# Packed columns for the third tile of 32 experts, its place in the order, and a subtraction in two pieces

## The reference

```python
E, K, F = (32, 4, 352);  FS = 1408;  CAP = 256
# every token goes to 4 of 32 experts; an expert takes at most 256 rows
buf = zeros((E, CAP + 1, H)).at[sorted_e, dest].set(x[tok])[:, :CAP]
g = einsum('ech,ehf->ecf', buf, w_gate)
u = einsum('ech,ehf->ecf', buf, w_up)
y = einsum('ecf,efh->ech', silu(g) * u, w_down)
out = zeros((T, H)).at[tok].add(y[sorted_e, pos] * wv)
out = out + sigmoid(x @ w_shared_gate) * (silu(x @ sw_gate) * (x @ sw_up) @ sw_down)
```

## Time and profile before

| | us |
|---|---|
| median of 3 runs | 1687.3 (1687.01 to 1688.22) |
| the profiled execution | 1695.61 |
| its span, first to last instruction | 1693.8 |
| TensorE matmuls busy | 1647.0 |
| VectorE busy | 1272.6 |
| GpSimd busy | 836.7 |
| ScalarE busy | 697.7 |

### The profile page before, as it was taken

One profiled execution on the slowest core, in us unless ns is written; L12 is line 12 of the kernel. 1 busy time (PEld: TensorE's weight loads), 2 busy tenths in 40 slices (PEclk: granted clock), 3 DMA queues, 4 the chain that ended last, 5 costly groups with the idle time before them and its releaser, 6 DMA issues.

```text
span 1693.8 us, 26093 instructions
## 1 busy us (share of the span) xinstructions
PE 1647.0 (97%) x8512; PEld 1402.2 (83%) x8512; DVE 1272.6 (75%) x1863; ACT 697.7 (41%) x1216; POOL 836.7 (49%) x691
## 2 busy tenths in 40 slices
PE   6999999998999999999998999999999999999999
PEld 4777888876999999999986788888788888888887
DVE  7989999997756555655579687676777768687776
ACT  5746555653766666666653212121221212112121
POOL 4587777774444444444457444251433525243351
PEclk9999999999999999999999999999999999999999
DMA  4544343424766666666687655454545343433431
GB/s 156 194 155 174 125 156 141 149 100 181 253 240 244 239 241 234 228 228 230 239 278 230 234 176 162 174 182 148 179 143 178 104 155 119 155 107 114 166 99 52
DMA packets 122420, 299.06 MB, mean 177 GB/s; under 512 B 19996, under 2 KB 31260, under 8 KB 117728
## 3 DMA queue, kind: packets, MB, share of 16 engines
q1 hardware_dynamic: 103104, 263.82, 43.6%
q0 software_dynamic: 18944, 33.66, 6.9%
q10 hardware_dynamic: 288, 0.52, 0.1%
HBM read 233.34 MB, written 81.35 MB: 186 GB/s over the span
## 4 chain that ended last, share of the span: by engine, by line
PE 74%; DVE 15%; issue 6%; ACT 2%; POOL 2%; another core or an unknown queue 0%; DMA 0%; DVEq 0%; POOLq 0%; ACTq 0%; SPq 0%
PE bank L2176 25%; PE bank L1400 16%; PE bank L2190 13%; PE bank L1427 8%; PE bank L2207 5%; PE bank L1024 4%; DVE mixf L719 3%; PE bank L1392 2%; DVE bank L687 1%; DVE st L667 1%; DVE mix L726 1%; DVE zT_lo L694 1%; DVE s_wg L2027 1%; PE bank L958 1%; DVE sr L740 1%
## 5 line engine op out<-in xcount | busy, mean ns | idle before, releaser
L1024 PE MATMUL bank<-mix,w 128*128 128x512 f32 x1488 | 353.7, 394 | 12.8 <-DVE ekv L735 7.6
L1024 PEld LDWEIGHTS bank<-mix,w 128*128 128x128 f32 x1488 | 277.0, 189 | 76.3 <-DVE ekv L735 5.8
L2176 PE MATMUL bank<-s_zT,s_wu 128*128 128x512 f32 x1056 | 256.7, 392 | 9.9 <-DVE bank L1932 9.9
L2190 PE MATMUL bank<-s_wd,s_h 128*128 128x512 f32 x1056 | 254.0, 390 | 1.1 <-DVE s_h L1938 1.1
L2176 PE MATMUL bank<-s_zT,s_wg 128*128 128x512 f32 x1056 | 253.7, 389 | 0.0
L2176 PEld LDWEIGHTS bank<-s_zT,s_wu 128*128 128x128 f32 x1056 | 199.5, 189 | 53.4 <-issue 11.9
L2190 PEld LDWEIGHTS bank<-s_wd,s_h 128*128 128x128 f32 x1056 | 198.4, 188 | 42.9 <-DVE s_h L1938 1.7
L2176 PEld LDWEIGHTS bank<-s_zT,s_wg 128*128 128x128 f32 x1056 | 198.2, 188 | 41.1
L1210 POOL TENSOR_TENSOR e_wg<-e_g_in,e_wg 128x1408 fp32r<-128x1408 f32 x31 | 100.7, 3249 | 212.6 <-ACT e_wg L1234 212.6
L1707 POOL DMA_INDIRECT s_picked<-y_rows,s_slot x128 | 140.6, 1099 | 78.3 <-DVE s_total L1988 39.1
L1816 ACT ACTIVATE s_act_g<-bank 128x512 f32<-128x512 f32 x88 | 52.5, 597 | 288.6 <-PE bank L2176 282.2
(11 more groups left out here) (188 smaller groups left out, 2489.3 us busy)
## 6 DMA issues: line engine op xcount, KB each, us to landing
s_wu<-wu_split SPq DMA_DIRECT2D x77, 512.0 KB
e_g_in<-in_w_gate SPq DMA_DIRECT2D x32, 704.0 KB
e_u_in<-in_w_up SPq DMA_DIRECT2D x32, 704.0 KB
e_d_in<-in_w_down SPq DMA_DIRECT2D x32, 512.0 KB
y_rows<-e_y SPq DMA_DIRECT2D x32, 512.0 KB, 2.9
s_zT<-zT_parts SPq DMA_DIRECT2D x16, 1024.0 KB, 6.8
zT_parts<-zT_hi SPq DMA_DIRECT2D x8, 1024.0 KB
zT_parts<-zT_lo SPq DMA_DIRECT2D x8, 1024.0 KB
```

Of the source, the lines that this page charges most:

```text
L1024: last = pe.matmul(pj[m][:], w[i][:, w_part, k, m * P:(m + 1) * P], mix[:, i % 2, k, x_part, :], start=(k == 0 and q == 0), stop=(k == KC ...
L2176: last = pe.matmul(into[:], w[:, w_part, k, :], zT[:, x_part, k, :], start=(q == 0 and k == 0), stop=(q == 2 and k == KC - 1))
L2190: last = pe.matmul(yp[j][:], h[:, i, h_part, j * P:(j + 1) * P], wd[f][:, w_part, :], start=(f == 0 and q == 0), stop=(f == NFS - 1 and q ...
```

## The change

**Packed columns.** The gate weights come from the host as 384 columns: the 352 of the gate and the last 32 (`UB`) of up. So the third tile of the gate group has 128 columns and yields 96 gate columns and 32 up columns. The other 64 (`UA`) up columns of the third tile lie in a tile of their own, `e_wua`, with 64 high columns and 64 low ones side by side. `product_third` multiplies these 128 columns by x low and by x high, 8 matmuls in place of 12. The result has the high weights' product in PSUM partitions 0 to 63 and the low weights' in 64 to 127. ScalarE copies the latter and the 32 columns from the gate group to a new tile `e_third` (`keep_third`, two instructions), VectorE adds the former to its first 64 partitions, and the product with the silu then reads `e_third` in place of the bank. An expert has 68 matmuls for gate and up.

**Order.** The packed tile is first (`ORDER` = 2, 0, 1); the transposes of the next rows stand between the second and the third `up_gate`. On ScalarE the scaled copies (`rows_hi`) come ahead of the last silu, and `up_hi` is two instructions (256 and 1024 columns). On VectorE `up_lo`, two instructions as well, goes from behind the first product to behind the last low part, and `rows_lo` ahead of the last product. GpSimd's gate low part is two instructions of 768 columns in place of one of 1408. Two tiles change their place in SBUF (`e_y1`, and those whose width changed).

```diff
 FT = [(f, min(P, F - f)) for f in range(0, F, P)]
+WHOLE = F // P * P
+UA = 64
+UB = F - WHOLE - UA
+FIRST, SECOND = F + UB, F - UB
...
-    wg = [at("e_wg0", [P, 2, KC * F], 0, F32R), at("e_wg1", [P, 2, KC * F], 96, F32R)]
-    wu = [at("e_wu0", [P, 2, KC * F], 128, F32R), at("e_wu1", [P, 2, KC * F], 270, F32R)]
+    wg = [at("e_wg0", [P, 2, KC, FIRST], 0, F32R), at("e_wg1", [P, 2, KC, FIRST], 96, F32R)]
+    wu = [at("e_wu0", [P, 2, KC * WHOLE], 128, F32R), at("e_wu1", [P, 2, KC * WHOLE], 270, F32R)]
+    wua = [at("e_wua0", [P, KC, 2, UA], 144, F32R), at("e_wua1", [P, KC, 2, UA], 286, F32R)]
...
-    y = [at("e_y0", [P, NCT, C], 308), at("e_y1", [P, NCT, C], 22)]
+    third = at("e_third", [P, CAP], 24)
+    y = [at("e_y0", [P, NCT, C], 308), at("e_y1", [P, NCT, C], 120)]
...
+    ORDER = (NF - 1, *range(NF - 1))
+    GATES = NF + 1
...
@@ -1207,8 +1224,12 @@
             pool.wait_ge(wg_hi, e + 1)
             if isinstance(e, int) and e == 1:
                 pool.wait_ge(wg_lo, 1)
-            pool.tensor_tensor(wg[half][:, 1, :], g_in[half][:], wg[half][:, 0, :].bitcast(F32),
-                               ALU.subtract).then_inc(wg_lo, 1)
+            whole, hi, lo = g_in[half][:], *(wg[half][:, i].rearrange("p k f -> p (k f)") for i in range(2))
+            piece = whole.shape[1] // 2
+            for i in range(2):
+                at = slice(i * piece, (i + 1) * piece)
+                last = pool.tensor_tensor(lo[:, at], whole[:, at], hi[:, at].bitcast(F32), ALU.subtract)
+            last.then_inc(wg_lo, 1)
...
         def up_hi(e, half, uses):
             act.wait_ge(u_loaded[half], uses * 16)
-            act.activation(wu[half][:, 0, :], u_in[half][:], ACT.Copy).then_inc(wu_hi, 1)
+            wait(act, y_done, (e - 1) * NCT)
+            act.activation(wua[half][:, :, 0, :], u_third(half), ACT.Copy)
+            act.activation(wu[half][:, 0, :], u_in[half][:, 0:KC * WHOLE], ACT.Copy).then_inc(wu_hi, 1)
...
-        def silu(e, f):
+        def silu(e, at):
...
             act.activation(act_g[0:m, f, :], gu[f][0:m, 0, :], ACT.Silu).then_inc(silu_made, 1)
 
-        def hidden_hi(e, f):
+        def keep_third(e):
+
+            act.wait_ge(up_done, e * NF + 1)
+            wait(act, h_made, gated(e - 1, 0) if not isinstance(e, int) or e else 0)
+            act.activation(third[0:UA, :], gu[2][UA:2 * UA, 1, :], ACT.Copy)
+            act.activation(third[UA:UA + UB, :], gu[2][P - UB:P, 0, :], ACT.Copy).then_inc(silu_made, 1)
+
+        def hidden_hi(e, at):
+            f = ORDER[at]
...
@@ -1273,19 +1305,21 @@
             if more:
                 gate_hi(e + 1, 1 - half, other)
             silu(e, 0)
+            keep_third(e)
             if more:
                 up_hi(e + 1, 1 - half, other)
             else:
                 output_early[0]()
+            silu(e, 1)
             hidden_hi(e, 0)
-            silu(e, 1)
             if not more:
                 output_early[1]()
             hidden_hi(e, 1)
+            if more:
+                rows_hi(e + 1, 1 - half)
             silu(e, 2)
             hidden_hi(e, 2)
             if more:
-                rows_hi(e + 1, 1 - half)
                 down_hi(e + 1, 1 - half, other)
...
         def up_lo(e, half):
             dve.wait_ge(wu_hi, e + 1)
-            dve.tensor_tensor(wu[half][:, 1, :], u_in[half][:], wu[half][:, 0, :].bitcast(F32),
+            dve.tensor_tensor(wua[half][:, :, 1, :], u_third(half), wua[half][:, :, 0, :].bitcast(F32), ALU.subtract)
+            dve.tensor_tensor(wu[half][:, 1, :], u_in[half][:, 0:KC * WHOLE], wu[half][:, 0, :].bitcast(F32),
                               ALU.subtract).then_inc(wu_lo, 1)
...
-        def hidden(e, f):
+        def hidden(e, at):
+            f = ORDER[at]
             m = FT[f][1]
-            dve.wait_ge(silu_made, e * NF + f + 1)
-            dve.tensor_tensor(act_g[0:m, f, :], act_g[0:m, f, :], gu[f][0:m, 1, :], ALU.mult).then_inc(h_made, 1)
-
-        def hidden_lo(e, f):
+            dve.wait_ge(silu_made, gated(e, at))
+            if at == 0:
+                dve.tensor_tensor(third[0:UA, :], third[0:UA, :], gu[f][0:UA, 1, :], ALU.add).then_inc(h_made, 1)
+                dve.wait_ge(h_made, e * GATES + 1)
+            up = gu[f][0:m, 1, :] if at else third[0:m, :]
+            dve.tensor_tensor(act_g[0:m, f, :], act_g[0:m, f, :], up, ALU.mult).then_inc(h_made, 1)
+
+        def hidden_lo(e, at):
+            f = ORDER[at]
             m = FT[f][1]
-            dve.wait_ge(h_hi, e * NF + f + 1)
...
@@ -1348,19 +1389,19 @@
             if more == 2:
                 make_index(e + 2, half, uses + 1)
             hidden(e, 0)
-            if more:
-                up_lo(e + 1, 1 - half)
-            else:
+            if not more:
                 output_early[0]()
+            hidden(e, 1)
             hidden_lo(e, 0)
-            hidden(e, 1)
             if not more:
                 output_early[1]()
             hidden_lo(e, 1)
+            if more:
+                rows_lo(e + 1, 1 - half)
             hidden(e, 2)
             hidden_lo(e, 2)
             if more:
-                rows_lo(e + 1, 1 - half)
+                up_lo(e + 1, 1 - half)
...
         def product(e, half, f, which, w):
-            f0, m = FT[f]
             for q, (w_part, x_part) in enumerate(PRODUCTS):
                 for k in range(KC):
-                    last = pe.matmul(gu[f][0:m, which, :], w[half][:, w_part, k * F + f0:k * F + f0 + m],
+                    last = pe.matmul(gu[f][:, which, :], w(half, w_part, k, f),
...
-        def up_gate(e, half, f):
-            if f == 0:
+        def product_third(half):
+
+            for x_part in (1, 0):
+                for k in range(KC):
+                    last = pe.matmul(gu[NF - 1][:, 1, :], wua[half][:, k].rearrange("p q f -> p (q f)"),
+                                     xT[half][:, x_part, k, :], start=(x_part == 1 and k == 0),
+                                     stop=(x_part == 0 and k == KC - 1))
+            return last
+
...
+        def up_gate(e, half, at):
+            f = ORDER[at]
+            if at == 0:
                 pe.wait_ge(x_lo, (e + 1) * KC)
                 pe.wait_ge(wg_lo, e + 1)
-            wait(pe, h_made, (e - 1) * NF + f + 1)
...
-            if f == 0:
+            wait(pe, h_made, gated(e - 1, at) if not isinstance(e, int) or e else 0)
+            if at and isinstance(e, int) and e == 0:
+                pe.wait_ge(shared["gate_made"], B * KC - 4 + at)
+            product(e, half, f, 0, gate_weight)
+            if at == 0:
                 pe.wait_ge(wu_lo, e + 1)
-            product(e, half, f, 1, wu).then_inc(up_done, 1)
+            (product(e, half, f, 1, up_weight) if at else product_third(half)).then_inc(up_done, 1)
...
-            for f in range(NF):
+            for at, f in enumerate(ORDER):
...
         def one_expert(e, half, more, uses):
-            for f in range(NF):
-                up_gate(e, half, f)
+            up_gate(e, half, 0)
+            up_gate(e, half, 1)
             if more:
                 turn(e + 1, 1 - half, uses + half)
+            up_gate(e, half, 2)
             down(e, half)
...
+    up = np.asarray(inputs["L0_ffn_w_up"])
+    give("w_first", np.concatenate([np.asarray(inputs["L0_ffn_w_gate"]), up[:, :, F - UB:]], axis=2))
+    up = up.reshape(E, P, KC, F)
+    give("w_second", np.concatenate([up[:, :, :, 0:WHOLE].reshape(E, P, KC * WHOLE),
+                                     up[:, :, :, WHOLE:F - UB].reshape(E, P, KC * UA)], axis=2))
```

41 lines of the change are left out of this document (24 added, 17 removed).

## The result

| | us | ratio to before [95%] |
|---|---|---|
| before, median of 5 runs beside it | 1688.22 (1687.01 to 1689.12) | |
| changed kernel, 5 runs | 1678.59 (1678.08 to 1679.94) | 0.9945 [0.9931, 0.9958] |
| the same kernel again, 5 runs | 1679.23 (1677.29 to 1679.81) | 0.9945 [0.9932, 0.9959] |
| forecast | 1672.6 (1670.5 to 1677.0) | |

A forecast was written before the change was run, and what follows sets the result against it. TensorE's back-to-back products were taken to bound the expert stage: 31 x 0.474 = 14.7 us saved, 0.1 lost in the first expert, say -14.7 from the 1687.3 median, giving 1672.6 us; range 1670.5 to 1677.0, 8 times in 10.

The forecast's parts named there:

- the term that prices the products: TensorE, gate and up: 68 products instead of 72 at 118.4 ns each, saving 0.474 us an expert, 14.7 us over 31.
- Rival 4: Packed tile: its eight products cost more than 118.4 ns, 178 each to cancel the saving; about 1687 us; chance 2%.
- Rival 2: TensorE, gate and up: weight loads set the pace, saving only 0.15 us an expert, 4.9 in all; 1682.4 us; chance 2%.
- TensorE bound, nothing in between: Expert stage: the chain holds TensorE alone without waits, 13.62 us an expert before, 13.15 after, so fewer instructions mean less time.
- The schedule: Other engines within an expert: last low part done at 10.98 us, wanted at 11.68, slack 0.70; added work costs 0.
- rival 1: Last low part of h overruns its 0.70 us slack; each 0.1 us beyond costs 3.2 in all, 0.2 gives 1679; chance 9%.
- The packed product: VectorE's product of the packed tile reads two tiles, so waits for GpSimd's second piece: 5.93 to 6.35 us.
- Rival 3: VectorE's two-tile instructions also wait for GpSimd's gathers; TensorE waits 1.4 us an expert, +29, so 1716 us; chance 3%.
- The first expert: Start of the expert stage: VectorE late, last low part at 446.7 against a wanted 446.6; loss 0.1 us, at most 0.5.
- The last expert and the output's first round: End of the expert stage: the last expert's own saving is worth nothing; the GpSimd and VectorE mixture after it 0, within 1.5 us.

The follow-up runs named there:

- before_384: Kernel before the change, with the gate weights' slices 384 columns apart instead of 352 and y1 moved; 1688.16 us (10 runs), ratio 1.0003.
- the padded kernels: Changed kernel with 32 unused columns behind each gate and up slice, in the second kernel the packed tile too; 1675.50 and 1675.44 us, ratios 0.9925 and 0.9928.

## Why the prediction was right in kind and wrong in size

**The failed step** is the term that prices the products: "The new products are all 128 wide and all 256 long, as those of the first tile, so I price them at the same 118.4 ns." Shape was the same, place was not. The change that made room for 32 up columns moved every slice from 1408 bytes apart to 1536, 1024 and 512. That price was also applied to the 48 products I held to be untouched, and all 68 went to 120.0 ns: 68 x 1.6 = 0.11 us an expert, 3.4 us in 31. The saving measured by stage is 13.62 - 13.253 = 0.367 us an expert, 11.0 in thirty. `before_384` shows the loss on the gate's 128-column products without the change, the padded kernels show the change without the loss, and their 1675.4 us lie inside the range. That spacing sets the pace is shown; why it does is open. What should have made me try it is that the diff turns 352 into 384 in a tile that TensorE reads 36 times an expert. Rival 4 looked at product price, but only for the eight packed ones. Rival 2 is refuted: loads as the pace would have given 0.15 us an expert, and 0.37 came.

**TensorE bound, nothing in between**: right. In a stage of 410.9 us it has no wait, and 68 products are there.

**The schedule**: right to 0.1 us, slack 0.82 for 0.70, so rival 1 didn't come. The packed product, which comes during GpSimd's second piece, waits for it and takes 1.94 us, as the earlier trace rows had it. The Trainium skill (SBUF — State Buffer, section Who interferes with whom) has whoever comes first hold the shared port for its whole instruction, and the trace agrees: 1.90 us in the median, 0.42 where GpSimd does not read. All its instances (least, median and most ns), beside those that read a bank:

```profile
L1379 DVE TENSOR_TENSOR e_act_g<-e_act_g,bank x64: 403/410/423, 435.6 to 848.2; 128x256 f32<-128x256 f32 x64
L1379 DVE TENSOR_TENSOR e_act_g<-e_act_g,e_third x32: 422/1900/1946, 435.3 to 843.6; 96x256 f32<-96x256 f32 x32
```

The 422 is the last expert's, where GpSimd makes no gate part. Rival 3 is refuted by the low parts beside gathers, which kept 411 to 428 ns.

**The first expert**: forecast, a loss of 0.1 us against the new period; measured, 13.45 against 13.25, so 0.2.

**The last expert and the output's first round**: I took 0 within 1.5. The last expert became 0.37 us shorter for TensorE and the round behind it 0.8 to 1.2 longer (115.93 and 115.49 us in the two profiles of the changed kernel, 114.71 in before), a loss of 0.4 to 0.8 net. VectorE came to the last low part 849.10 - 839.31 = 9.79 us behind the start, 9.88 before: inside the forecast 9.8 to 10.3. What follows it differs. VectorE in before:

```profile
867.93 1.22 DVE L1955 TENSOR_TENSOR_SCAN s_b_sum<-keep_decay,s_ek 128x512 f32<-128x512 f32 x1
869.07 1.20 DVE L1957 TENSOR_TENSOR_SCAN s_a_sum<-keep_decay,s_ekv 128x512 f32<-128x512 f32 x1
870.18 1.26 DVE L2027 TENSOR_TENSOR s_wg<-s_ahead,s_wg 128x512 fp32r<-128x512 f32 x2
```

In the changed kernel, VectorE and then GpSimd:

```profile
850.05 1.22 DVE L2012 TENSOR_TENSOR_SCAN s_b_sum<-keep_decay,s_ek 128x512 f32<-128x512 f32 x1
851.18 2.25 DVE L2014 TENSOR_TENSOR_SCAN s_a_sum<-keep_decay,s_ekv 128x512 f32<-128x512 f32 x1
853.36 2.31 DVE L2084 TENSOR_TENSOR s_wg<-s_ahead,s_wg 128x512 fp32r<-128x512 f32 x2
```

```profile
850.89 1.47 POOL L1801 TENSOR_TENSOR s_wu<-s_piece,s_wu 128x512 fp32r<-128x512 f32 x1 [3.39 <-ACT s_wu L1925]
852.32 2.20 POOL L1798 TENSOR_TENSOR s_wd<-s_piece,s_wd 128x512 fp32r<-128x512 f32 x1
```

Before, GpSimd's subtraction took 5.73 us, with VectorE passing ahead of it; now GpSimd gets in and takes 1.47 and 2.20, and VectorE's scan and pair of subtractions take 1.05 us more each. The other profile of the changed kernel shows the same (GpSimd 2.16 and 2.21, the scan 2.25). No run tests it by itself, and what decides who passes is not shown.

**The account.** Forecast -14.7; product pace +3.4; the ends +0.4 to +0.8; together -10.5 to -10.9, against the measured -9.6. The traces agree with that, with 10.5 from the first expert to the end. The 0.9 to 1.3 left over are less than single runs of one kernel differ by (1677.3 to 1679.8), and no stage of the traces shows them. Against the forecast's number comes 0.9 more, since before's median was 1687.3 in its three runs and 1688.2 beside the changed kernel. My own range (1671.0 to 1674.5) allowed for the ends and for nothing in the 2176 products that carry the sum: 1% of their price is 2.6 us.

**A better version.** 32 unused columns in the first and up tiles, or 16 in all three, give 1675.5 and 1675.4 us, 0.2% under the changed kernel and 0.7 to 0.8% under before.

## What to carry to other kernels

When one engine's back-to-back instructions are the whole path, price each by where its operands lie as well as by shape, and let the range hold a per cent of that price. Whoever packs more columns into a weight tile should look at what the row length became: here multiples of 256 bytes went with 1.4% on the products of 128 columns, and a few unused columns gave it back; it is to be tried, since no rule for it came out of these runs. An order of steps off the path is worth what the waits on the path show, here some 0.5 us in two experts of 32; but half of such an order can cost more than all of it gives. And a single run that is 3 us off is looked up in its trace, stage by stage with the clock, before a cause is given to it.
